# A routed two-layer block on one core: nine of forty expert tiles cut to 128 rows, reads and pads moved in the DMA order

## The chip, the cores and the metric

The kernel runs on one NeuronCore of a Trainium2 chip. Its engines each take their own instructions in order and meet at semaphores: TensorE (PE; its weight loads PEld), VectorE (DVE), ScalarE (ACT), GpSimd (POOL), and SyncE (SP), which here only issues DMAs. The metric is the device time of one execution in microseconds, as a median over runs.

## The reference, cut to what matters

Two layers follow each other on 4096 tokens (32 sequences of 128) of 256 numbers. Each layer has a 16-head cross-attention to a context, and then a feed-forward part in which each token goes to the best two of eight experts.

```
x = x + tanh(g_xattn[0]) * attention0(layernorm(x), ctx)
x = x + tanh(g_ffn[0])   * experts0(layernorm(x))        # relu(x W1 + b1) W2 + b2, hidden 1024
x = x + tanh(g_xattn[1]) * attention1(layernorm(x), ctx, mask)
x = x + tanh(g_ffn[1])   * experts1(layernorm(x))        # (silu(x Wg) * (x Wu)) Wd, hidden 512
```

Each layer so has 8192 rows of expert work (two per token), and their split over the experts is known only while the kernel runs.

## The kernel before, in words

A product in full precision is made of three in the fast format: every operand is cut into a rounded part ("high") and a rest ("low", the original less the rounded part), and `three` (L466 to L470) adds high by high, high by low and low by high. So each operand costs a rounding copy on ACT and a subtraction on DVE or POOL.

The attention of a layer runs in 128 steps (`FIRST`, `START`). While it runs, the router ranks the tokens of each of 8 groups, and POOL scatters their rows by indirect DMAs (L1554) into a buffer in memory, sorted by expert. The last of these steps (`late`, up to `LAST`) lie among the first 13 expert tiles.

The experts take the sorted rows in tiles of `TS` = 256 rows, `NT` = 39 tiles in a layer. Each tile belongs to one expert. The first `KE` = 16 are listed after six groups (`dve_lists_early`); the other 23 after all eight (`dve_lists`, L1366, three parts from step `LIST1` = 171). The 23 are as many as the worst split needs. Tiles past the last real one repeat it, and their rows are scattered out of bounds, so that nothing is written. Behind each expert's rows `pad` (L855) writes 256 rows that point nowhere, so that a tile may read past the end.

Per tile i the engines do this, each in its own order:

- PE (`pe_experts`, L687): turns the rows of tile i+1 (`pe_turn_x`, four transposes, L638), then the up products of tile i in four groups q (`pe_up`, 48 matmuls of 256 columns), then the down products of tile i-1 in two halves (`pe_down`, 48 matmuls in layer 0, 24 in layer 1). "Iteration i" below is this stretch, from one group of L638 to the next.
- ACT (`act_experts`, L915): in layer 1 the scaling of tile i-2's output (`act_y`, L882); the rounding of weight quarter 3 of tile i-1 (`act_w`, L865); relu with bias (L895) or silu (L898) of each group; the rounded hidden part (L906, L908); the rounded rows (L871); and quarters 0 and 1 of tile i+1 and quarter 2 of tile i.
- DVE (`dve_experts`, L1461): in layer 0 the output plus bias of tile i-2 (`dve_y`, L1440); the rests of the hidden parts (L1446, L1449); in layer 1 silu times up (`dve_gated`, L1455); the rests of the rows (L1417); and by `low_w` (L1413) the rests of weight quarters 1 and 2.
- POOL (`pool_experts`, L1584): `low_w` of quarter 3 of tile i-1, the late scatters, two scatters of tile i-2's output rows (`pool_y`, L1579, in layer 1 L1581), and `low_w` of quarter 0 of tile i+1.
- SP (`sp_experts`, L1728): the DMAs, in one order: rows of tile i+2 (`sp_fetch_x`, L1635), in layer 0 two biases, then weight quarter 3 of tile i, quarters 0 and 1 of tile i+2, quarter 2 of tile i+1. The raw quarters have one buffer each, so a fetch waits until the rest of the quarter before it is made. At tile 13 (`KE - 3`) SP issues all eight pads in a row, and in layer 0 at tile 18 three weight reads and two context reads for the next layer.

The weights' rounded parts and rests (`WH`, `WL`) exist once: the up half may be replaced when the up products that read it are done, and so with the down half. The rows' buffer `xt` and the rounded rows `XS` exist twice.

Of the kernel before, what the change touches and what calls it, by code (L numbers as in the profile page):

```python
# [6 lines left out]
F32 = mybir.dt.float32  # L7
# [8 lines left out]
T = B * S  # L16
E = 8
# [5 lines left out]
NT = (2 * T - E) // TS + E  # L23
GE, KE = 6, 16
assert KE <= -(-(2 * GE * G * S - E * (TS - 1)) // TS)
# [20 lines left out]
C_TOK = C_TILE + NT - KE  # L46
# [4 lines left out]
def constants():  # L51
# [9 lines left out]
    c[:, C_TILE:C_TILE + NT - KE] = np.arange(NT - KE)  # L61
# [52 lines left out]
LIST0, TX, LIST1 = 116, (124, 126), 171  # L114
# [51 lines left out]
def step(s, name):  # L166

    for b in range(B):
        if s == (START + LATE_AT[name][b] if b in LATE_AT[name] else 4 * b + AT[name]):
            return b  # L170
    return None

# [7 lines left out]
def program(nc, A):  # L180
    ctx = ExitStack()
    with ctx:  # L182
# [60 lines left out]
        tl = sb("tl", [128, 4, E])  # L243
        tli = sb("tli", [128, 2, E], I32)
# [62 lines left out]
        tile2 = [(L, i, a) for L in LL for i in range(NT) for a in range(2)]  # L307

# [13 lines left out]
        d_fy = [mark(f"d_fy{r}", [k for k in tile2 if k[1] % 2 == r], 16) for r in range(2)]  # L322
# [132 lines left out]
        def experts_out(w, L):  # L455

            w.wait_ge(*m_dn[L, NT - 1, 1])
            w.wait_ge(*m_y[L][L, NT - 1, 1])
            w.wait_ge(*v_h[L, NT - 1, 3])
            w.wait_ge(*p_w3[L, NT - 1])  # L460
            w.wait_ge(*d_fy[(NT - 1) % 2][L, NT - 1, 1])
            w.wait_ge(*d_fy[NT % 2][L, NT - 2, 1])
# [169 lines left out]
        def pe_turn_x(e, w, L, i):  # L632
            bank = place[L, "tx", i]
            w.wait_ge(*d_fx[i % 2][L, i])
            bank_free(w, L, "tx", i)
            for t in range(2):
                for a in range(2):
                    ins = e.transpose(bank[:, t * 256 + a * 128:t * 256 + (a + 1) * 128], xt[:, i % 2, a, t * 128:(t + 1) * 128], ident)  # L638
            ins.then_inc(*m_x(L, i))

        def pe_up(e, w, L, i, q):
            w.wait_ge(*v_x[L, i])
            w.wait_ge(*l_w[q // 2][L, i])
            if i:
                w.wait_ge(*(v_h[1, i - 1, q] if L else a_h[0, i - 1, q]))
            else:
                w.wait_ge(*(a_p[L, NU - 3], a_p[L, NU - 2], a_p[L, NU - 1], a_pt[L, NU - 1])[q])
            for z in range(2):
                f = q if L else 2 * q + z
                for t in range(2):  # L650
                    c = t * (F0, F1)[L] + f * 128 + z * L * 2 * F1
                    ins = three(e, HBK[q][:, z * 256:z * 256 + 256], (WH[:, c:c + 128], WL[:, c:c + 128]),
                                (XS[i % 2][:, 0, t * 256:t * 256 + 256], XS[i % 2][:, 1, t * 256:t * 256 + 256]), t == 0, t == 1)
            ins.then_inc(*m_h(L, i, q))

        def pe_rows(e, w, L, i, f, a):
            nf, c = NFs[L], (2 * F0, 4 * F1)[L] + f * D
            w.wait_ge(*v_h[L, i, f if L else f // 2])
            w.wait_ge(*l_w[2 + 2 * f // nf][L, i])
# [3 lines left out]
        def pe_down(e, w, L, i, half):  # L663
            nf = NFs[L]
            if i:
                w.wait_ge(*m_y[L][L, i - 1, 1])
# [3 lines left out]
            for f in range(half * nf // 2, (half + 1) * nf // 2):  # L670
                for a in range(2):
                    ins = pe_rows(e, w, L, i, f, a)
            ins.then_inc(*m_dn(L, i, half))

        def pe_down_last(e, w, L):

            w.wait_ge(*m_y[L][L, NT - 2, 1])
            for a in range(2):
                for f in range(NFs[L]):
                    ins = pe_rows(e, w, L, NT - 1, f, a)  # L680
                ins.then_inc(*m_dn(L, NT - 1, a))
# [5 lines left out]
        def pe_experts(e, w, L):  # L687
# [13 lines left out]
            pe_down_last(e, w, L)  # L701
# [143 lines left out]
        def act_attention(e, w, L):  # L845
            act_first(e, w, L)
            for s in range(FIRST, START):
                act_step(e, w, L, s)
                for i in range(2):
                    if s == TX[0] + i:  # L850
# [16 lines left out]
        def act_turn_x(e, w, L, i):  # L867
# [3 lines left out]
            e.activation(XS[i % 2][:, 0], place[L, "tx", i][:, :], ACT.Copy).then_inc(*a_x(L, i))  # L871

        def act_y(e, w, i):

            w.wait_ge(*v_xi[1, i])
            if i >= 2:
                w.wait_ge(*d_fy[i % 2][1, i - 2, 1])
            else:
                w.wait_ge(*v_xup[1, B - 1])
            for a in range(2):  # L880
                w.wait_ge(*m_dn[1, i, a if i == NT - 1 else 1])
                e.activation(yo[:, i % 2, a], YB[a][:, 0:D], ACT.Copy, scale=xg[:, i % 4, a:a + 1]).then_inc(*a_y(1, i, a))  # L882

        def act_hidden(e, w, L, i, q):
            r = i % 2
# [954 lines left out]
```

## Time and profile before

| what | value |
|---|---|
| median of 3 runs | 1677.26 us (1676.21 to 1680.76) |
| profiled execution | 1675.83 us, its span 1674.0 us |
| mean granted TensorE clock | 0.973 |
| PE, ACT, DVE, POOL busy share | 93%, 74%, 73%, 50% |
| DMA, mean over the span | 153 GB/s |
| layer 0 experts | first group of L638 at 358.51 us, the last at 837.83 us |
| layer 1 experts | first group of L638 at 1244.78 us, the last at 1639.40 us |

The share of a busy engine is read per stage: an engine is the bound of a stage if it stands idle nowhere in it. A timeline row gives in brackets the idle time of the engine before the instruction and what ended it.

### The profile page before, as it was taken

Reading aid. Unit: us, or ns where it says so; the run is one execution under the profiler, and the core shown is the slowest. Engines: PE = TensorE matmul, PEld = TensorE weight load, DVE = VectorE, ACT = ScalarE, POOL = GpSimd, SP = SyncE. Lnnn points to the kernel's source line nnn. Section 1 sums busy time; section 2 is a strip of 40 time slices with the busy share of each in tenths; the row PEclk is TensorE's granted clock in tenths of the full one; section 3 lists DMA queues with packets and bytes.
Section 4 is the critical chain, followed back from the end, with each engine's and each line's share of the span. In section 5 each row is a group of like instructions: output and inputs, shape, how many; then the busy total and the mean of one; then the engine's idle time right before and its main releaser. Section 6 shows DMA issues by size and latency. Waiting matters only on the chain. (4 is left out here: it accounts for less than half of the span.)

```text
span 1674.0 us, 37438 instructions
## 1 busy us (share of the span) xinstructions
PE 1548.8 (93%) x12728; PEld 1404.1 (84%) x12728; DVE 1218.4 (73%) x2778; ACT 1234.4 (74%) x2854; POOL 844.1 (50%) x907
## 2 busy tenths in 40 slices
PE   7999999989999899999988999999989887899996
PEld 5788888869999899999986777777769876899996
DVE  5677777758899677777857788888766867566663
ACT  5888888878877678888854877777777655677774
POOL 4124444345677465555551123333335677677776
PEclk9999999999999999999999999999989998899999
DMA  3212222147677887777742223333246667888783
GB/s 112 54 50 75 76 77 77 52 132 211 206 238 221 228 275 212 231 222 229 231 128 64 71 85 104 103 109 106 61 133 191 164 183 203 219 218 234 224 226 97
DMA packets 208990, 256.57 MB, mean 153 GB/s; under 512 B 29555, under 2 KB 156788, under 8 KB 208800
## 3 DMA queue, kind: packets, MB, share of 16 engines
q1 hardware_dynamic: 187040, 219.53, 44.8%
q0 software_dynamic: 21120, 34.39, 8.1%
q8 instruction: 101, 1.65, 0.4%
q14 instruction: 89, 0.73, 0.1%
q10 hardware_dynamic: 640, 0.26, 0.1%
HBM read 194.53 MB, written 45.74 MB: 144 GB/s over the span
## 5 line engine op out<-in xcount | busy, mean ns | idle before, releaser
L1413 POOL TENSOR_TENSOR KXR<-U,KXR 128x1024 fp32r<-128x1024 f32 (+1 forms) x156 | 356.1, 2285 | 270.1 <-ACT KXR L865 247.4
L468 PE MATMUL ps<-QR,KXR 128*128 128x256 f32 x1248 | 365.2, 293 | 21.7 <-POOL KXR L1413 9.7
L469 PE MATMUL ps<-QR,KXR 128*128 128x256 f32 x1248 | 357.1, 286 | 0.0
L470 PE MATMUL ps<-QR,KXR 128*128 128x256 f32 x1248 | 357.1, 286 | 0.0
L865 ACT ACTIVATE KXR<-U 128x1024 fp32r<-128x1024 f32 (+1 forms) x312 | 288.9, 948 | 88.4 <-PE ps L470 44.3
L803 ACT ACTIVATE U<-ps,mx 128x128 f32<-128x128 f32 x1024 | 299.1, 405 | 17.3 <-DVE mx L1233 16.9
L468 PEld LDWEIGHTS ps<-QR,KXR 128*128 128x128 f32 x1248 | 243.9, 195 | 25.3 <-POOL KXR L1413 10.7
L469 PEld LDWEIGHTS ps<-QR,KXR 128*128 128x128 f32 x1248 | 243.8, 195 | 0.0
L470 PEld LDWEIGHTS ps<-QR,KXR 128*128 128x128 f32 x1248 | 243.2, 195 | 0.0
L1233 DVE TENSOR_REDUCE mx<-ps 128x4 f32<-128x512 f32 x256 | 174.3, 683 | 67.0 <-PE ps L470 35.4
L1413 DVE TENSOR_TENSOR KXR<-U,KXR 128x1024 fp32r<-128x1024 f32 (+1 forms) x156 | 195.0, 1281 | 24.3 <-ACT KXR L865 24.0
L546 PE MATMUL ps<-cst,U 128*128 128x128 f32 x1024 | 164.1, 284 | 11.7 <-DVE U L1243 10.4
L810 ACT ACTIVATE U<-ps 128x512 f32<-128x512 f32 x256 | 166.6, 651 | 6.7 <-PE ps L546 6.7
L1554 POOL DMA_INDIRECT xs_scr<-XR,PI x112 | 113.8, 1016 | 113.5 <-DVE PI L1142 85.6
L546 PEld LDWEIGHTS ps<-cst,U 128*128 128x128 f32 x1024 | 118.2, 144 | 49.3 <-issue 23.0
L895 ACT ACTIVATE U<-ps,b1s 128x256 f32<-128x256 f32 x312 | 130.3, 472 | 28.2 <-PE ps L470 28.2
L468 PE MATMUL ps<-KXR,PTR 128*128 128x256 f32 x480 | 137.6, 287 | 6.2 <-DVE U L1440 3.5
L1446 DVE TENSOR_TENSOR PTR<-U,PTR 128x512 fp32r<-128x512 f32 x80 | 93.5, 1194 | 65.3 <-ACT PTR L906 65.3
L469 PE MATMUL ps<-KXR,PTR 128*128 128x256 f32 x480 | 136.4, 284 | 0.0
L470 PE MATMUL ps<-KXR,PTR 128*128 128x256 f32 x480 | 136.3, 284 | 0.0
L1581 POOL DMA_INDIRECT out<-U,xi x78 | 123.7, 1586 | 20.8 <-issue 20.2
L468 PE MATMUL ps<-KXR,QR 128*128 128x512 f32 x256 | 123.3, 482 | 6.9 <-ACT U L803 3.6
(228 smaller groups left out, 3985.3 us busy)
## 6 DMA issues: line engine op xcount, KB each, us to landing
U<-in_wpack SPq DMA_DIRECT2D x234, 512.0 KB, 4.4
U<-in_wpack SPq DMA_DIRECT2D x78, 256.0 KB, 4.4
KXR<-U SPq DMA_DIRECT2D x504, 32.0 KB
U<-xs_scr SPq DMA_DIRECT2D x39, 258.0 KB, 4.5
U<-xs_scr SPq DMA_DIRECT2D x39, 257.0 KB, 4.6
U<-in_ctx_t SPq DMA_DIRECT2D x16, 512.0 KB, 5.9
U<-ys_scr SPq DMA_DIRECT2D x32, 256.0 KB, 3.2
U<-in_L_ffn_b SPq DMA_DIRECT2D x39, 128.0 KB
```

The source lines that it names most:

```text
L468: e.matmul(o, wh, xh, start=first, stop=False)
L469: e.matmul(o, wh, xl, start=False, stop=False)
L470: return e.matmul(o, wl, xh, start=False, stop=done)
L546: ins = e.transpose(bank[:, h * 128:(h + 1) * 128], PB[:, i % 3, h], ident)
L803: ins = e.activation(PB[:, i % 3, h], SB_[i % 3][:, h * 128:(h + 1) * 128], ACT.Exp, bias=mx[:, i % 4, h:h + 1], scale=-1.0)
L810: e.activation(PT[:, i % 3].rearrange("p h k -> p (h k)"), pt_place["p", i][:, :], ACT.Copy).then_inc(*a_pt(L, i))
L865: e.activation(w_cols(L, WH, n), w_raw(L, n), ACT.Copy).then_inc(*a_w[n](L, i))
L895: ins = e.activation(HB[:, r, f], HBK[q][:, z * 256:z * 256 + 256], ACT.Relu, bias=b1s[:, r, f:f + 1])
L1233: e.tensor_reduce(mx[:, i % 4], SB_[i % 3][:, :].rearrange("p (h k) -> p h k", h=4), AX.X, ALU.min).then_inc(*v_mx(L, i))
L1413: e.tensor_tensor(w_cols(L, WL, n), w_raw(L, n), hi, ALU.subtract).then_inc(*l_w[n](L, i))
L1554: e.indirect_dma_start(xs_d[L], bass.IndirectOffsetOnAxis(ap=PI[:, g % 2, z, j:j + 1], axis=0), xr(g)[:, z, j, 0:ROWS[L]], None).then_inc( ...
L1581: ins = e.indirect_dma_start(ys_d[1], at, yo[:, r, a, :], None, bounds_check=T - 1, oob_is_err=False, compute_op=ALU.add)
```

## The change

Of 40 tiles in each layer 31 hold 256 rows ("pairs" of halves) and nine hold 128 ("singles"): tiles 18, 21, 23, 26, 29, 31, 34, 37 and 39. The row slots of a layer go from 39 x 256 = 9984 to 31 x 256 + 9 x 128 = 9088. The lists name first the pairs, then the singles (`column` maps a tile to its place), in four parts with 40 small DVE instructions in place of three with 20.

For a single, the rounded rows and their rests lie side by side in one 256-column operand. The up products are then two matmuls per weight block instead of three: high by (high, rest) and low by (high, rest), 32 matmuls in all. The two halves of a bank are added afterwards: ACT copies the right half out (`act_part`, with the bias in layer 0), DVE adds the left (`dve_sum`). In layer 1 ACT then makes the silu (`act_gate`) and DVE the product from two SBUF operands. The product of low by rest, left out before, is now within the sum. The down products of a single take one half: 24 matmuls in layer 0, 12 in layer 1.

The rest of the edits: rows are read three tiles ahead instead of two, behind quarter 3; the first two tiles' rows are read behind all four quarters of tile 0, and tile 0's rows are turned one step later (`TX`); the pads go out four each at tiles 11 and 12, between the other reads; the five reads for the next layer go out one each at tiles 18 to 22; and in layer 1 the rest of quarter 3 of tiles 0 to 15 is made on DVE. `pe_down_last`, which did the last tile's two halves of rows one after the other, is dropped. The hidden buffers of even and odd tiles change places.

```diff
-NT = (2 * T - E) // TS + E
+NT, NPAIR = 40, 31
+SINGLES = (2, 5, 7)
-LIST0, TX, LIST1 = 116, (124, 126), 171
+LIST0, W0, TX, LIST1 = 116, 124, (125, 126), 171
+def single(i):
+    return i >= KE and (i - KE) % 8 in SINGLES
...
+        def l_w(L, i, n):
+            return v_w3 if n == 3 and L == 1 and i < KE else (p_w0, v_w1, v_w2, p_w3)[n]
...
         def pe_up(e, w, L, i, q):
+                    if single(i):
+                        o, xx = HBK[q][:, z * 256:z * 256 + 256], XS[i % 2][:, :, t * 128:t * 128 + 128]
+                        e.matmul(o, WH[:, c:c + 128], xx, start=t == 0, stop=False)
+                        ins = e.matmul(o, WL[:, c:c + 128], xx, start=False, stop=t == 1)
...
+        def act_part(e, w, L, i, q):
+            r, part = i % 2, HBK[q][:, :].rearrange("p (z n) -> p z n", z=2)[:, :, HALF:TS]
+            w.wait_ge(*m_h[L, i, q])
+            w.wait_ge(*v_h[L, i - 2, q])
+            if L == 0:
...
+                    ins = e.activation(HB[:, r, f, HALF:TS], part[:, z], ACT.Identity, bias=b1s[:, r, f:f + 1])
+            else:
+                ins = e.activation(HB[:, r, 4 + q].rearrange("p (z n) -> p z n", z=2), part, ACT.Copy)
+        def act_gate(e, w, i, q):
+            w.wait_ge(*v_s[1, i, q])
+            e.activation(HB[:, i % 2, 4 + q, 0:HALF], HB[:, i % 2, q, 0:HALF], ACT.Silu).then_inc(*a_h(1, i, q))
...
         def act_experts(e, w, L):
+                for q in range(4 if single(i) else 0):
+                    act_part(e, w, L, i, q)
+                    if q == 0 and i + 1 < NT:
+                        act_turn_x(e, w, L, i + 1)
+                    if q == 1 and i + 1 < NT:
+                        act_w(e, w, L, i + 1, 0)
+                    if L == 0 and q:
+                        act_hidden_high(e, w, 0, i, q - 1)
+                    if L == 1 and q:
+                        act_gate(e, w, i, q - 1)
+                    if L == 1 and q > 1:
+                        act_hidden_high(e, w, 1, i, q - 2)
...
+        def dve_sum(e, w, L, i, q):
+            r, part = i % 2, HBK[q][:, :].rearrange("p (z n) -> p z n", z=2)[:, :, 0:HALF]
+            w.wait_ge(*a_t[L, i, q])
+            if L == 0:
+                hb = HB[:, r, 2 * q:2 * q + 2]
+                ins = e.tensor_tensor(hb[:, :, 0:HALF], part, hb[:, :, HALF:TS], ALU.add)
+            else:
+                o, t = (HB[:, r, f].rearrange("p (z n) -> p z n", z=2) for f in (q, 4 + q))
+                ins = e.tensor_tensor(o, part, t, ALU.add)
         def dve_gated(e, w, i, q):
+            if single(i):
+                left, right = HB[:, r, 4 + q, 0:HALF], HB[:, r, q, HALF:TS]
...
         def dve_experts(e, w, L):
+                if L == 1 and 1 <= i <= KE:
+                    low_w(e, w, 1, i - 1, 3)
+                for q in range(4 if single(i) else 0):
+                    dve_sum(e, w, L, i, q)
+                    if q == 0 and i + 1 < NT:
+                        dve_turn_x(e, w, L, i + 1)
+                    if L == 0 and q:
+                        dve_hidden(e, w, 0, i, q - 1)
+                    if L == 1 and q:
+                        dve_gated(e, w, i, q - 1)
+                    if L == 1 and q > 1:
+                        dve_hidden(e, w, 1, i, q - 2)
...
         def pool_experts(e, w, L):
-                if i:
+                if i and (L == 0 or i > KE):
                     low_w(e, w, L, i - 1, 3)
...
         def sp_experts(e, w, L):
+            sp_fetch_x(e, w, L, 2)
             for i in range(NT):
+                x, m = 4 * (i - KE + 5), i - KE - 2
-                if i == KE - 3:
-                    for x in range(E):
-                        pad(e, w, L, x)
-                if L == 0 and i == KE + 2:
-                    sp_ahead(e)
-                    for g in range(2):
-                        sp_context(e, w, 1, g)
-                if i + 2 < NT:
-                    sp_fetch_x(e, w, L, i + 2)
...
                 if i:
                     sp_fetch(e, w, L, i, 3, sp_expert(e, w, L, i))
+                if x in (0, 4):
+                    pad(e, w, L, x)
+                if i + 3 < NT:
+                    sp_fetch_x(e, w, L, i + 3)
+                if x in (0, 4):
+                    pad(e, w, L, x + 1)
+                if L == 0 and 0 <= m < 3:
+                    sp_ahead(e, m)
+                if L == 0 and 3 <= m < 5:
+                    sp_context(e, w, 1, m - 3)
...
```

## Rows read from the trace of the kernel before

**Rows 1.** The page's first part, and one group of its fifth (count | busy us, mean ns).

```profile
PE 1548.8 (93%) x12728; PEld 1404.1 (84%) x12728; DVE 1218.4 (73%) x2778; ACT 1234.4 (74%) x2854; POOL 844.1 (50%) x907
...
L803 ACT ACTIVATE U<-ps,mx 128x128 f32<-128x128 f32 x1024 | 299.1, 405 | 17.3 <-DVE mx L1233 16.9
```

**Rows 2.** Stretches: length; busy PE, PEld, DVE, ACT, POOL (count); clock, DMA share, GB/s.

```profile
706.69:754.39 47.70, 47.70 (x403) 47.70 (x402) 35.85 (x41) 39.34 (x68) 28.31 (x16) 1.00 0.79 226
1512.37:1557.74 45.37, 45.37 (x383) 45.37 (x382) 31.56 (x66) 34.49 (x76) 34.20 (x20) 1.00 0.83 229
```

**Rows 3.** PE timeline at one boundary of layer 0 (start, us, engine, line).

```profile
718.36 0.28 PE L469 MATMUL ps<-KXR,WR 128*128 128x256 f32 x1
718.48 0.28 PE L470 MATMUL ps<-KXR,MK 128*128 128x256 f32 x1
718.59 0.60 PE L638 MATMUL ps<-cst,U 128*128 128x128 f32 x4
```

**Rows 4.** The view of rows 2, of disturbed iterations: two, two, two, two, one, one, one.

```profile
536.35:570.49 34.14, 26.26 (x202) 25.85 (x201) 19.42 (x19) 19.44 (x34) 16.41 (x9) 0.90 0.88 243
606.41:635.15 28.74, 25.57 (x202) 25.36 (x201) 21.25 (x23) 19.66 (x34) 14.63 (x8) 0.94 0.87 287
1407.12:1438.85 31.73, 19.90 (x154) 19.49 (x153) 14.88 (x27) 14.00 (x31) 16.41 (x9) 0.84 0.83 207
1377.33:1407.12 29.79, 22.40 (x154) 21.58 (x153) 25.14 (x63) 15.74 (x34) 22.77 (x17) 0.83 0.72 185
1339.31:1358.14 18.83, 12.58 (x92) 12.35 (x93) 6.51 (x15) 9.26 (x19) 16.61 (x12) 0.82 0.67 174
...
358.51:365.26 6.75, 5.12 (x38) 4.11 (x38) 2.98 (x6) 4.04 (x9) 0.52 (x1) 0.58 0.87 273
1244.78:1250.72 5.94, 4.85 (x33) 3.73 (x33) 2.04 (x5) 4.04 (x9) 0.37 (x1) 0.50 0.94 306
```

**Rows 5.** PE timeline: first transposes of three tiles, idle time and its releaser in brackets.

```profile
556.58 1.12 PE L638 MATMUL ps<-cst,U 128*128 128x128 f32 x4 [7.11 <-DMA U<-xs_scr]
...
1428.40 0.90 PE L638 MATMUL ps<-cst,U 128*128 128x128 f32 x3 [10.32 <-DMA U<-xs_scr]
...
621.65 0.66 PE L638 MATMUL ps<-cst,U 128*128 128x128 f32 x4 [3.17 <-DMA U<-xs_scr]
```

**Rows 6.** SP timeline of layer 0: the eight pads, and two neighbouring reads of a steady tile.

```profile
541.04 8.74 SPq L858 DMA_DIRECT2D xs_scr<-cst  x8
...
709.10 0.38 SPq L1635 DMA_DIRECT2D U<-xs_scr  x1
710.25 0.35 SPq L1616 DMA_DIRECT2D b1s<-in_wpack  x1
```

**Rows 7.** Timelines of a steady layer-1 iteration (from 1539.59): ACT one row, then POOL.

```profile
1540.60 0.63 ACT L865 ACTIVATE KXR<-U 128x512 fp32r<-128x512 f32 x1
...
1541.31 1.29 POOL L1413 TENSOR_TENSOR KXR<-U,KXR 128x512 fp32r<-128x512 f32 x1 [1.77 <-ACT KXR L865]
1542.76 1.55 POOL L1581 DMA_INDIRECT out<-U,xi  x1 [0.15 <-issue]
1544.61 1.55 POOL L1581 DMA_INDIRECT out<-U,xi  x1 [0.30 <-issue]
1545.62 2.99 POOL L1413 TENSOR_TENSOR KXR<-U,KXR 128x1024 fp32r<-128x1024 f32 x1
```

**Rows 8.** DVE instructions of two lines: duration in ns, least/median/most, first and last start.

```profile
L1446 DVE TENSOR_TENSOR PTR<-U,PTR x80: 658/692/3223, 369.9 to 857.3; 128x512 fp32r<-128x512 f32 x80
...
L1449 DVE TENSOR_TENSOR PTR<-ps,PTR x80: 410/420/426, 1258.6 to 1655.9; 128x256 fp32r<-128x256 f32 x80
```

**Rows 9.** POOL timeline of layer 1 during the late scatters.

```profile
1334.11 1.22 POOL L1554 DMA_INDIRECT xs_scr<-XR,PI  x1 [6.21 <-DVE PI L1142]
1335.36 1.29 POOL L1413 TENSOR_TENSOR KXR<-U,KXR 128x512 fp32r<-128x512 f32 x1
```

**Rows 10.** DVE timeline of layer 0: an instruction of the late list's first part.

```profile
512.21 2.99 DVE L1376 CAST tl<-tli 128x8 f32<-128x8 int32 x1
```

More of the change, by code:

```diff
@@ L45 @@
 C_TILE = C_LT + 64
-C_TOK = C_TILE + NT - KE
+C_TOK = C_TILE + max(KE, NPAIR - KE)
 C_PAD = C_TOK + 2 * B
@@ L171, in step, with halves, column @@
     return None
+def single(i):
+    return i >= KE and (i - KE) % 8 in SINGLES
+def halves(i):
+    return range(1 if single(i) else 2)
+def column(i):
+    if i < KE:
+        return i
+    n = sum(single(m) for m in range(i))
+    return NPAIR + n if single(i) else i - n
+assert sum(not single(i) for i in range(NT)) == NPAIR and single(NT - 1)
+assert 2 * NPAIR + NT - NPAIR == 2 * T // HALF + E - 1
 def late(i, k):
@@ L700, in pe_experts @@
                     pe_late(e, w, L, i, 2 + half)
-            pe_down_last(e, w, L)
+            for half in range(2):
+                pe_down(e, w, L, NT - 1, half)
         def act_weight(e, w, L, i):
@@ L1305, in dve_step @@
                     dve_lists_early(e, w, L, n)
-            for n in range(3):
+            for n in range(4):
                 if s == LIST1 + n:
@@ L1366, in dve_lists @@
         def dve_lists(e, w, L, part):
-            n, lt, ti = CR[:, B], cst[:, C_LT:C_LT + 64].rearrange("p (a b) -> p a b", a=E), cst[:, C_TILE:C_TILE + NT - KE]
+            n, lt, ti = CR[:, B], cst[:, C_LT:C_LT + 64].rearrange("p (a b) -> p a b", a=E), cst[:, C_TILE:C_TOK]
+            np_, nl = NPAIR - KE, NT - KE
+            pairs, ends, cuts, sums, over, rest, du, dp, ds = (tl[:, m] for m in range(9))
             if part == 0:
                 w.wait_ge(*v_c.now)
-                e.tensor_tensor(tl[:, 3], CR[:, B], cst[:, C_REG:C_REG + E], ALU.add).then_inc(*v_c.up())
-                e.tensor_scalar(tli[:, 0], n, float(TS - 1), None, ALU.add).then_inc(*v_c.up())
+                e.tensor_tensor(sums, CR[:, B], cst[:, C_REG:C_REG + E], ALU.add).then_inc(*v_c.up())
+                e.tensor_scalar(tli[:, 0], n, float(HALF - 1), None, ALU.add).then_inc(*v_c.up())
@@ new lines, in dve_lists @@
+                e.tensor_tensor(tlm[:, :, :], tl[:, 5:6, :].to_broadcast([128, E, E]), lt, ALU.mult).then_inc(*v_c.up())
+                e.tensor_scalar(du, du, float(TS), float(REG), ALU.mult, ALU.add).then_inc(*v_c.up())
+                w.wait_ge(*v_c.now)
+                e.tensor_reduce(sums, tlm[:, :, :], AX.X, ALU.add).then_inc(*v_c.up())
+                e.scalar_tensor_tensor(ds, rest, float(-HALF), du, ALU.mult, ALU.add).then_inc(*v_c.up())
+                w.wait_ge(*v_c.now)
+                e.tensor_scalar(pairs, ends, -1.0, None, ALU.add).then_inc(*v_c.up())
@@ L1571, in pool_y @@
             if i:
-                w.wait_ge(*d_fy[1 - r][L, i - 1, 1])
+                w.wait_ge(*d_fy[1 - r][L, i - 1, end(i - 1)])
             elif L == 1:
                 w.wait_ge(*d_out[NG - 1])
-            for a in range(2):
+            for a in halves(i):
                 w.wait_ge(*m_y[L][L, i, a])
@@ L1720, in sp_attention @@
                     v = sp_expert(e, w, L, 0)
-                    for n in range(2):
+                    for n in range(4):
                         sp_fetch(e, w, L, 0, n, v)
@@ L1724, in sp_attention @@
                         sp_fetch_x(e, w, L, i)
-                    for n in range(2, 4):
-                        sp_fetch(e, w, L, 0, n, v)
         def sp_experts(e, w, L):
```

224 lines of the change are left out of this document (138 added, 86 removed).

## The prediction

> **What bounds the kernel now.** The busy shares come first: PE 93%, no other engine above 74% [rows 1]. A share is a mean over stages, so the expert stages are read next, in stretches. In layer 0 four undisturbed iterations take 47.70 us and PE is busy for 47.70 of them, so an iteration is 11.92 us of PE; in layer 1 five take 45.37, all PE, 9.07 each [rows 2]. The reader is to see two things there: PE has no gap, and ACT comes second with 9.83 us an iteration in layer 0 and 6.90 in layer 1. The boundary gives the price of one matmul of 256 columns, 0.12 us from start to start [rows 3]: 96 of them at 0.119 make 11.42 in layer 0 and the turn of the next rows the other 0.5; 72 make 8.57 in layer 1, and the turn 0.5.
>
> Then the disturbed iterations. A pair of layer 0 takes 34.14 where two quiet ones take 23.84, another 28.74; in layer 1 there are pairs of 31.73 and 29.79 where two take 18.14, and one iteration of 18.83 [rows 4]. The PE timeline says what ends the idle time: rows of a tile that are not there, with 7.11, 10.32 and 3.17 us of idleness [rows 5]. The clock falls with it: 0.82 to 0.94 in all these stretches, against 1.00 in quiet ones, so 1.2 GHz for a part of each.
>
> **The change part by part.** The sum is made against the profiled execution, 1675.83 us (a span of 1674.0 and 1.83 around it); the median of the runs shown is 1.4 more.
>
> *Singles, PE alone.* A single has 32 up matmuls, and 24 down in layer 0 or 12 in layer 1, all of 256 columns: 56 x 0.119 + 0.25 (two transposes instead of four) = 6.9 us, and 44 x 0.119 + 0.25 = 5.5. Nine singles replace eight pairs. Layer 0: 9 x 6.9 - 8 x 11.92 = -33. Layer 1: 9 x 5.5 - 8 x 9.07 = -23.
>
> *Singles in layer 0, with the others.* An iteration with a single's up and a pair's down is 0.45 + 3.8 + 5.7 = 10.0 us of PE; the next, with a pair's up and a single's down, 9.0. The pair's ACT work is 9.83 and does not shrink, so behind each single ACT is up to 1 us late, and the quarters of weights come after it. A single's ACT work: four quarters 4, eight copies of 128 columns at 0.29 (299.1 over 1024, [rows 1]) 2.3, roundings and the turn about 1.8, together 8.1, so it catches up in the iterations that hold one. DMA: a pair moves 226 GB/s x 11.92 us = 2.7 MB [rows 2], a single about 0.25 less (half of the rows in and out), so five pairs and three singles 20.8 MB in 80 us, 260 GB/s; one stretch has 287 at a share of 0.87 [rows 4], so it fits. I take 5 us of the 33 as lost: -28. Bounds: -33, and 0 if every single costs what a pair costs per unit replaced (9 at 10.6).
>
> *Singles in layer 1, with the others.* Here a chain stands beside PE that the change does not shorten. From the boundary at 1539.59: ACT scales the output, then rounds quarter 3 (1540.60); POOL makes its rest (1541.31), two scatters, and from 1545.62 the rest of quarter 0, which ends at 1548.61 [rows 7]. That is 9.02 us after the boundary, and the next up products, at 9.07 + 0.4, need it. PE has 0.4 us of slack today. With a single's up and a pair's down PE needs 0.46 + 3.81 + 2.86 = 7.1 us, while the chain still has a pair's two scatters: PE waits 0.9 to 1.5. In the next iteration PE needs 7.6, but ACT comes late to the chain's first step: a single gives it about 7.8 us (four copies, four silus, four roundings on top of the same quarters), and its last product and rounding wait for DVE. The DVE row without a PSUM operand reaches from 658 to 3,223 ns, the one with it stays between 410 and 426 [rows 8]; the single's product reads SBUF twice, and POOL's rest of quarter 0 lies in the same microseconds, so the last of its products may be held for up to 2.99 us. So the chain starts 2 to 3.5 late, and PE waits another 1.2 to 2.8. I take 3.2 for both waits together: 9 x 3.2 = 29. Waits of this length are where the clock may fall: in the iteration of 18.83 the shortfall is 0.18 x 18.83 = 3.4 us of full speed [rows 4], half of it beside an idle PE; 1.7 us each for four of the waits, 7. Sum: -23 + 36 = +13. Bounds: -23 (all hidden) and +31 (6 us a single).
>
> The Trainium skill (GPSIMD Engine Reference, section Specifications) says that GpSimd shares its SBUF interfaces with VectorE and contends with DVE instructions that have two SBUF inputs. By that rule the old product, which read PSUM, was free of it and each of the new ones may be held, so all nine singles would stand at the upper end of the 2 to 3.5 us and the sum at 1631; without the rule they stand at the lower end and the sum at 1621. The two lines of [rows 8] agree with it.
>
> *Pads.* The eight pads take SP from 541.04 to its next read at 550.61 [rows 6], and the rows queued behind them come 7.11 and 10.32 late [rows 5]. Cost now: 34.14 - 23.84 = 10.3 in layer 0 and 31.73 - 18.14 = 13.6 in layer 1 [rows 4]. Spread by four, each adds 1.15 us of SP (709.10 to 710.25, [rows 6]) to an iteration with 7 reads in layer 0 and 5 in layer 1, so 12.7 and 10.4 us of SP against 11.9 and 9.1: about 1 us late, in iterations that are longer than that anyway. What is late next are tile 16's rows, which wait for the last pad to land and hold quarters 0 to 2 of later tiles behind them. I take 3 us back: -21. Bounds: -24 and -8.
>
> *Rows three ahead, reads spread.* The rows were issued 2.4 us into an iteration for the next one; now they have a whole iteration more. The stretch with the five extra reads costs 28.74 - 23.84 = 4.9 [rows 4], and layer 1 has some 3 us of shorter waits for rows. -8; bounds 0 and -8.
>
> *First tile.* The first tile's iteration has a clock of 0.58 in layer 0 and 0.50 in layer 1 [rows 4]: PE waits for rows that follow the landing of the scatters. Turning them one step later puts one attention step of about 3 us in front of that wait, and the quarters no longer queue behind it: -5; bounds 0 and -10.
>
> *Quarter 3 on DVE.* In layer 1 POOL stands before a scatter for 6.21 us while a ready rest of 1.29 is queued behind it [rows 9]; the iteration of 18.83 [rows 4] comes of that. The change takes 1.29 from POOL and adds 0.7 to DVE, which makes the numbers that the scatter waits for. -3; bounds -10 and +3.
>
> *The lists.* Twenty more small DVE instructions a layer at about 0.2, half of them in a chain; one of the old ones took 2.99 behind POOL [rows 10]. The first part stands in front of `dve_y` in layer 0. +3; bounds 0 and +6.
>
> *The end.* The last tile is a single: its down products are in the sum above; one scatter of 1.55 less: -2.
>
> Sum: -28 + 13 - 21 - 8 - 5 - 3 + 3 - 2 = -51. 1675.8 - 51 = 1625, against the median 1626.
>
> **The rivals.**
> A: PE stays the bound in layer 1 too, the singles save 18 instead of losing 13. For: POOL is busy only 6.8 of 9.07 us an iteration there. Against: the chain of [rows 7] has 0.4 us of slack. 1626 - 31 = 1595.
> B: the singles save nothing in layer 0 as well, by ACT's order or by the reads: 1626 + 28 = 1654. For: ACT's 9.83 beside 9.0. Against: 10.0 of PE on the other side of it.
> C, the slower one: the hand-overs between ACT and DVE inside a single. If in both layers two of a single's four groups are held for 2.99, as the worst row of L1446 shows, each of the 18 singles costs 6 us above PE's time: 1676 - 56 - 36 + 108 = 1692. It decides from 5.1 us a single on, where the 92 us of gains are spent. Against it: the sums read PSUM, like the line that stays at 410 to 426 [rows 8], and up products and down products of a tile lie an iteration apart.
> D: the reads do not come earlier, because the rows' wait on the turn of two tiles before is what holds them: pads and reads give 5 instead of 29: 1650.
>
> **How the numbers follow.** Forecast 0.50, A 0.20, B 0.15, D 0.09, C 0.06. The likeliest gives 1626 us. A reaches below and B and D above; the range 1594 to 1657 takes them in and leaves out C and the outer ends of A. The measurement tells 0.3%, 5 us, from no change. Faster are the forecast, A, B and D, 0.94; of C 0.02 falls within 0.3% and 0.04 beyond it, slower.
>
> **What would show it.** Right: in layer 0 iterations of about 10.0 and 9.0 us around each single with PE nearly always busy; in layer 1 waits of PE for POOL's L1413 (now another line) of 1 to 3 us behind each single, and a granted clock below 1.00 there; no wait for rows above 1 us; tiles 14 to 16 as long as their neighbours. Wrong: layer-1 iterations of 7.1 and 7.6 without waits (A); layer-0 iterations of 11 to 12 behind singles (B); DVE instructions of a single with 2 us and more (C); waits for rows as before (D).

## The result, and the profile after

The changed kernel takes 1663.5 us (median of 4 runs, 1661.6 to 1667.6) against 1677.1 before: a ratio of 0.992, interval 0.989 to 0.994. It is faster by 13.6 us (0.8%), where the forecast was 51, and lies 37 us above the predicted time.

First the page's busy shares of the kernel after, as in [rows 1]:

```profile
PE 1507.7 (91%) x12256; PEld 1357.2 (81%) x12256; DVE 1289.6 (77%) x2920; ACT 1224.8 (74%) x2913; POOL 819.7 (49%) x881
```

PE lost 41 us of work and only 8.5 us of span, so waits took the place of products. DVE is busy for 71 us more. Both are told apart by stretches. The view is that of [rows 2] (length; busy PE, PEld, DVE, ACT, POOL; clock, DMA share, GB/s), cut at the turns of tiles 0, 14, 18 and the last one of layer 0, then of tiles 0, 11 and 17 of layer 1, and the end. Before:

```profile
358.51:536.35 177.84, 167.64 (x1387) 164.84 (x1387) 147.18 (x243) 137.35 (x241) 112.87 (x81) 0.97 0.71 210
536.35:594.35 58.00, 50.12 (x403) 49.71 (x401) 39.94 (x38) 38.47 (x68) 30.77 (x17) 0.94 0.85 239
594.35:837.83 243.48, 240.31 (x2003) 240.03 (x2002) 186.63 (x205) 197.09 (x341) 142.53 (x80) 0.99 0.79 233
1244.78:1367.80 123.02, 106.11 (x848) 102.26 (x849) 84.56 (x223) 80.50 (x167) 76.10 (x60) 0.94 0.67 187
1367.80:1447.92 80.12, 60.80 (x459) 59.23 (x458) 54.64 (x130) 43.63 (x95) 50.75 (x33) 0.87 0.77 198
1447.92:1674.03 226.11, 211.97 (x1770) 211.19 (x1768) 143.65 (x297) 159.65 (x348) 162.47 (x96) 0.98 0.73 202
```

After:

```profile
359.49:539.02 179.53, 167.85 (x1383) 165.74 (x1383) 151.24 (x262) 135.41 (x235) 113.45 (x80) 0.97 0.71 208
539.02:588.97 49.95, 48.24 (x403) 47.81 (x402) 38.26 (x42) 39.08 (x68) 30.17 (x16) 1.00 0.90 262
588.97:817.46 228.49, 217.32 (x1790) 215.07 (x1789) 204.69 (x232) 186.59 (x354) 145.47 (x77) 0.99 0.84 249
1225.79:1340.69 114.90, 102.89 (x844) 99.91 (x845) 88.30 (x233) 76.81 (x160) 62.88 (x50) 0.97 0.72 199
1340.69:1412.60 71.91, 60.25 (x459) 58.97 (x458) 52.72 (x155) 44.89 (x96) 41.92 (x26) 0.93 0.79 217
1412.60:1665.47 252.87, 203.84 (x1576) 199.13 (x1574) 187.09 (x347) 162.03 (x390) 158.68 (x90) 0.93 0.67 182
```

The reader is to see three things. The pads' stretches (the second and the fifth) are 8 us shorter each. The one with layer 0's singles (the third, 21 iterations in place of 20) is 15 us shorter. The one with layer 1's (the last) is 27 longer: PE has 8 us less work there, and 49 us outside of its work instead of 14, DVE is busy for 187 us instead of 144, and the clock is 0.93.

PE's waits, by what ended them (total us, times, longest; "issue" is a wait whose releaser the trace doesn't name):

```profile
PE ps L503 <- issue: 32.7, 15, 4.5
PE ps L503 <- POOL KXR L1515: 13.6, 7, 4.6
PE ps L691 <- issue: 12.6, 6, 3.3
...
PE ps L675 <- DMA U<-xs_scr: 8.7, 2, 4.4
```

The waits for rows of [rows 5] are gone but for the first tile of each layer (two, 4.4 at most). Of the 21 unnamed ones 17 stand ahead of an iteration's first up product in the tiles from the first single on; the other four lie in the pads' stretches. Where they end is seen by laying the engines' timelines side by side. Layer 0:

```profile
664.07 0.60 PE L675 MATMUL ps<-cst,U 128*128 128x128 f32 x4
667.66 2.41 POOL L1515 TENSOR_TENSOR KXR<-U,KXR 128x1024 fp32r<-128x1024 f32 x1 [5.17 <-ACT KXR L900]
670.23 1.25 POOL L1720 DMA_INDIRECT ys_scr<-U,xi  x1 [0.15 <-issue]
671.79 1.44 POOL L1720 DMA_INDIRECT ys_scr<-U,xi  x1 [0.30 <-issue]
673.24 2.37 POOL L1515 TENSOR_TENSOR KXR<-U,KXR 128x1024 fp32r<-128x1024 f32 x1
...
675.71 0.35 PE L503 MATMUL ps<-QR,KXR 128*128 128x256 f32 x1 [2.19 <-issue]
```

Layer 1, two iterations that follow one another:

```profile
1486.40 2.39 POOL L1515 TENSOR_TENSOR KXR<-U,KXR 128x1024 fp32r<-128x1024 f32 x1 [1.22 <-ACT KXR L900]
1486.55 2.40 DVE L1579 TENSOR_TENSOR ps<-U 128x128 f32<-128x128 f32 x1 [0.73 <-ACT U L953]
1488.99 0.28 ACT L963 ACTIVATE PTR<-ps 128x128 fp32r<-128x128 f32 x1 [2.00 <-DVE ps L1579]
...
1498.11 4.16 POOL L1515 TENSOR_TENSOR KXR<-U,KXR 128x1024 fp32r<-128x1024 f32 x2
1501.13 0.36 PE L503 MATMUL ps<-QR,KXR 128*128 128x256 f32 x1 [3.08 <-issue]
```

In layer 0 PE starts 0.10 us after GpSimd's rest of quarter 0 (673.24 + 2.37 = 675.61), which stood behind two scatters. The chain began late: GpSimd's rest of quarter 3 starts 3.6 us after the boundary (667.66 - 664.07), where it starts 1.4 us after it in the kernel before (719.99 - 718.59, below). In layer 1 a single's product, 0.29 us elsewhere, takes 2.40 beside such a rest; ScalarE waits 2.00 for it; and an iteration later the rest of quarter 0 (the first of the two at 1498.11) comes 3.08 us late for PE.

### The profile page after: what moved, and what is told of

Same layout as the page of the kernel before. It is cut to its first block and busy times, and to the rows that moved or that the text cites. A ratio compares the mean times of both kernels' runs of the same rounds, so it can differ in the third digit from the quotient of the medians.

```text
span 1665.5 us, 36632 instructions
## 1 busy us (share of the span) xinstructions
PE 1507.7 (91%) x12256; PEld 1357.2 (81%) x12256; DVE 1289.6 (77%) x2920; ACT 1224.8 (74%) x2913; POOL 819.7 (49%) x881
## 5 line engine op out<-in xcount | busy, mean ns | idle before, releaser
L1515 POOL TENSOR_TENSOR KXR<-U,KXR 128x1024 fp32r<-128x1024 f32 (+1 forms) x144 | 342.2, 2402 | 240.0 <-ACT KXR L900 239.2
L900 ACT ACTIVATE KXR<-U 128x1024 fp32r<-128x1024 f32 (+1 forms) x320 | 296.1, 948 | 75.0 <-DMA U<-in_wpack 51.3
L503 PE MATMUL ps<-QR,KXR 128*128 128x256 f32 x992 | 295.8, 298 | 59.3 <-issue 32.7
L504 PE MATMUL ps<-QR,KXR 128*128 128x256 f32 x992 | 288.4, 291 | 0.0
L505 PE MATMUL ps<-QR,KXR 128*128 128x256 f32 x992 | 288.3, 291 | 0.0
L1515 DVE TENSOR_TENSOR KXR<-U,KXR 128x1024 fp32r<-128x1024 f32 (+1 forms) x176 | 232.8, 1354 | 26.8 <-ACT KXR L900 26.3
L503 PEld LDWEIGHTS ps<-QR,KXR 128*128 128x128 f32 x992 | 197.7, 199 | 68.1 <-issue 48.6
L504 PEld LDWEIGHTS ps<-QR,KXR 128*128 128x128 f32 x992 | 198.2, 200 | 0.0
L505 PEld LDWEIGHTS ps<-QR,KXR 128*128 128x128 f32 x992 | 197.8, 199 | 0.0
L581 PE MATMUL ps<-cst,U 128*128 128x128 f32 x1024 | 163.2, 283 | 11.9 <-DVE U L1315 10.6
L1722 POOL DMA_INDIRECT out<-U,xi x71 | 116.9, 1646 | 54.8 <-issue 25.0
L503 PE MATMUL ps<-KXR,WR 128*128 128x256 f32 x444 | 127.3, 287 | 6.4 <-DVE U L1544 6.4
L503 PE MATMUL ps<-KXR,QR 128*128 128x512 f32 x256 | 123.5, 482 | 8.1 <-ACT U L838 4.8
L504 PE MATMUL ps<-KXR,WR 128*128 128x256 f32 x444 | 126.2, 284 | 0.0
L503 PE MATMUL ps<-KXR,PTR 128*128 128x256 f32 x408 | 116.5, 285 | 5.0 <-POOL KXR L1515 2.0
L931 ACT ACTIVATE U<-ps,b1s 128x256 f32<-128x256 f32 x248 | 103.1, 470 | 20.1 <-PE ps L505 18.9
L504 PE MATMUL ps<-KXR,PTR 128*128 128x256 f32 x408 | 115.7, 284 | 0.0
```

The source lines that it names most:

```text
L503: e.matmul(o, wh, xh, start=first, stop=False)
L504: e.matmul(o, wh, xl, start=False, stop=False)
L505: return e.matmul(o, wl, xh, start=False, stop=done)
L581: ins = e.transpose(bank[:, h * 128:(h + 1) * 128], PB[:, i % 3, h], ident)
L900: e.activation(w_cols(L, WH, n), w_raw(L, n), ACT.Copy).then_inc(*a_w[n](L, i))
L931: ins = e.activation(HB[:, r, f, 0:n], HBK[q][:, z * 256:z * 256 + n], ACT.Relu, bias=b1s[:, r, f:f + 1])
```

## The experiments

Two questions: what each part of the change is worth, and what takes the singles' gain. Theory 1: VectorE's instructions with two SBUF operands are held by GpSimd's rests, and only the short iterations feel it. Rivals: the longer way over ScalarE and VectorE in a single, and GpSimd's queue. Lines and tiles are named as in the changed kernel. Behind each time stands its ratio to the kernel before, run beside it, with a 95% interval. The kernel before took 1673.3 to 1677.1 us in the different groups of runs, so a difference of two medians from different groups is good to about 4 us.

**Without singles.** A flag for each layer; without it the layer has 39 pairs and the lists of before, all else is the change.

```diff
+SING = (0, 0)
+NTS = tuple(40 if s else 39 for s in SING)
...
-    return i >= KE and (i - KE) % 8 in SINGLES
+    return SING[L] and i >= KE and (i - KE) % 8 in SINGLES
```

> All of the change except the singles: 39 pairs in both layers, the lists of before. Theory 1 (GpSimd's rests hold VectorE, and only the short iterations of singles feel it): what is left keeps the gains read off the trace after, about 11 us in layer 0 and 12 in layer 1, so about 1653. Rival (the prediction's sum without its singles: -21 -8 -5 -3, and +2 for the end): about 1642.

1644.6 us, 0.981 (0.980 to 0.983): 19 us faster than with the singles. The gain of 32 us is near what the prediction's terms give for this part (-21 -8 -5 -3 = -37, or 35 with the 2 us for the end). Its stretches:

```profile
359.07:533.92 174.85, 165.34 (x1383) 162.76 (x1383) 146.89 (x241) 135.16 (x235) 112.90 (x80) 0.99 0.72 213
533.92:584.73 50.81, 48.65 (x403) 47.90 (x402) 40.99 (x41) 39.35 (x69) 30.03 (x17) 1.00 0.88 250
584.73:823.19 238.46, 238.46 (x2002) 238.46 (x2001) 185.15 (x204) 196.58 (x340) 143.54 (x80) 1.00 0.81 239
1231.62:1346.73 115.11, 104.24 (x845) 101.51 (x845) 87.41 (x233) 76.98 (x160) 62.55 (x50) 0.95 0.73 200
1346.73:1417.76 71.03, 58.84 (x458) 57.60 (x457) 51.92 (x135) 44.72 (x96) 42.37 (x26) 0.95 0.80 221
1417.76:1642.86 225.10, 211.68 (x1770) 211.19 (x1768) 144.18 (x298) 158.91 (x348) 161.01 (x95) 0.99 0.73 202
```

**Singles in layer 0 alone** (`SING = (1, 0)`).

> Singles in layer 0 alone, layer 1 with 39 pairs. By the stages of the two traces the singles save about 9 us in layer 0 with its end and cost about 20 in layer 1: about 1644, faster than the changed kernel by 20 us. The prediction's terms would give 1642 - 28 = 1614; its rival B (singles save nothing in layer 0) the same as the run without singles.

1638.1 us, 0.978 (0.976 to 0.980). So the singles bring 6.6 us in layer 0 and cost 25.4 in layer 1 (1663.5 - 1638.1).

**Thin rests.** GpSimd's rests of quarters 0 and 3 on a few columns; the low parts of those weights are left as the layer's first tile made them.

```diff
-            e.tensor_tensor(w_cols(L, WL, n), w_raw(L, n), hi, ALU.subtract).then_inc(...)
+            o, raw = w_cols(L, WL, n), w_raw(L, n)
+            if i and l_w(L, i, n) in (p_w0, p_w3):
+                o, raw, hi = (t[:, 0:1, 0:16] if n < 2 else t[:, 0:16] for t in (o, raw, hi))
+            e.tensor_tensor(o, raw, hi, ALU.subtract).then_inc(...)
```

> The changed kernel with GpSimd's rests of quarters 0 and 3 cut to 16 or 16 columns of one block for all tiles but the first of a layer (the rest of the low parts of these weights is not computed again); every wait and every signal stays. Theory 1 (these rests hold VectorE's instructions with two SBUF operands for 2.4 to 3.3 us): the holds go, PE's waits of 1.3 to 3.1 us around the singles go in both layers, about 1625. Rival (ACT is late, because a single's way over ACT and VectorE is longer than a pair's): at most 8 us, 1655 to 1663, PE's waits stay at 1.5 to 3.

1569.1 us, 0.936 (0.935 to 0.938): 94 us less than the changed kernel, far more than expected. The two stretches with singles:

```profile
575.71:788.86 213.15, 213.15 (x1791) 213.15 (x1790) 136.74 (x238) 187.62 (x357) 48.41 (x77) 1.00 0.87 268
...
1360.29:1567.36 207.07, 191.09 (x1576) 188.43 (x1574) 137.88 (x347) 160.56 (x390) 79.23 (x90) 0.98 0.82 224
```

In layer 0 PE is busy for the whole stretch. A single passes as many instructions between ScalarE and VectorE here as in the changed kernel, so that way by itself is not the bound: this rival falls. Thin rests shorten GpSimd's queue as well as the holds, so this run does not tell these two apart.

**All rests on VectorE.** The same work, done elsewhere:

```diff
+RESTS = ((0, 3), (0, 3))
...
+        def on_v(L, i, n):
+            return n in (1, 2) or i > 0 and n in RESTS[L] or n == 3 and L == 1 and i < KE
...
+                if i and on_v(L, i - 1, 3):
+                    low_w(e, w, L, i - 1, 3)
...
+                    if q == 2 and i + 1 < NTS[L] and on_v(L, i + 1, 0):
+                        low_w(e, w, L, i + 1, 0)
```

> The changed kernel with the rests of quarters 0 and 3 on VectorE for all tiles but a layer's first, so GpSimd does no rest beside the experts. VectorE gains 0.96 + 0.96 (0.7 in layer 1) us of work an iteration and loses the holds of about 5 us in layer 0 and 2 to 3 in layer 1. Theory 1: 1630 to 1645. Rival (what counts is how many instructions VectorE and ACT have to pass one another, not the holds): VectorE's extra work makes the singles longer, 1665 to 1680.

1593.0 us, 0.951 (0.949 to 0.952), 70 less than the changed kernel and again far below the expectation. About 24 us of the gain lie ahead of the singles: the first stretch of layer 0 takes 167.3 us instead of 179.5, and the two of layer 1 take 106.2 and 67.6 instead of 114.9 and 71.9, while the pads' stretch of layer 0 takes 1 us more. So it is not true that only the short iterations feel GpSimd's rests, as theory 1 had it. (A rest of 1024 columns takes VectorE 1.22 us, not the 0.96 expected.) Then the same **without singles**, which gives their worth where GpSimd does no rest:

> No singles, and the rests of quarters 0 and 3 on VectorE. Theory 1: without holds the singles are worth what PE saves less what is left of waits: in the run with the rests on VectorE layer 0's stretch with singles took 217 us where twenty pairs take 238, layer 1's 176 against 181, so this kernel is 27 us slower than that one, 1620, and 25 faster than without singles alone (1645), from the first 17 tiles of both layers. Rival (the rests on VectorE help by themselves and the singles bring nothing): 1593 to 1600.

1628.3 us, 0.973 (0.972 to 0.975). The stretches of layer 0's and layer 1's singles, first with singles, then with pairs:

```profile
577.48:794.69 217.21, 214.37 (x1790) 213.34 (x1789) 177.89 (x278) 187.99 (x357) 45.82 (x35) 1.00 0.86 263
...
1371.93:1588.64 216.71, 195.46 (x1576) 189.32 (x1574) 174.24 (x395) 160.15 (x391) 69.89 (x43) 0.98 0.79 215
```

```profile
576.69:815.16 238.47, 238.47 (x2003) 238.47 (x2002) 176.86 (x242) 196.68 (x340) 63.60 (x40) 1.00 0.79 235
...
1399.19:1623.88 224.69, 211.55 (x1770) 211.14 (x1768) 173.23 (x344) 157.30 (x349) 78.53 (x50) 0.98 0.74 204
```

Here the singles are worth 35 us (1628.3 - 1593.0): 21 in the stretch of layer 0 and 8 on the way from it to layer 1 (403.5 against 411.5), 8 in layer 1. VectorE, with 101 us of rests in that stretch of layer 0, is busy for less of it than in the changed kernel (178 us against 205).

**The product from PSUM.** In layer 1 the sum goes back to PSUM and the silu reads it there (not shown), so a single's product has one SBUF operand:

```diff
-                o, t = (HB[:, r, f].rearrange("p (z n) -> p z n", z=2) for f in (q, 4 + q))
-                ins = e.tensor_tensor(o, part, t, ALU.add)
+                t = HB[:, r, 4 + q].rearrange("p (z n) -> p z n", z=2)
+                ins = e.tensor_tensor(part, part, t, ALU.add)
...
-                left, right = HB[:, r, 4 + q, 0:HALF], HB[:, r, q, HALF:TS]
+                left, right = HB[:, r, 4 + q, 0:HALF], up
```

> The changed kernel; in layer 1 a single's sum is written back to PSUM, so its product has one SBUF operand as a pair's has. GpSimd's rests stay. If the held product is what makes layer 1's singles slow, as the prediction had it, most of the 25 us goes: about 1640. If the rest of quarter 1 on VectorE, held behind two rests of GpSimd in a row, is the wait that ends last: 3 to 10 us, 1653 to 1660, and PE's waits of about 3 us behind each single stay.

1640.1 us, 0.981 (0.978 to 0.983), what the held product was to give. GpSimd's work and order are those of the changed kernel. The groups of layer 1's last stretch (count | busy us, mean ns | idle before), the changed kernel first:

```profile
L1579 DVE TENSOR_TENSOR ps<-U 128x128 f32<-128x128 f32 x36 | 34.9, 968 | 6.5 <-ACT U L953 6.5
```

```profile
L1579 DVE TENSOR_TENSOR ps<-U,ps 128x128 f32<-128x128 f32 x36 | 10.5, 291 | 8.7 <-ACT U L953 8.7
```

24.4 us of the product's holds are gone, and 23.4 us of time (19 by the two ratios to the kernel before). That the two numbers agree so well is in part luck, since other holds moved too: VectorE's rests of 1024 columns (quarter 1) took 39.8 us in this stretch instead of 54.1, those of 512 columns 26.5 instead of 18.9. The stretch falls from 253 us to 227, as long as with pairs (225) and still 20 above the thin rests (207).

**One rest each.** `RESTS = ((3,), (3,))`, then `((0,), (0,))`:

> The change's own step carried on: quarter 3's rest on VectorE for all tiles of both layers, GpSimd keeps quarter 0's. Theory 1: half of the held time goes, and two rests of GpSimd never follow one another: 1620 to 1635. Rival (VectorE's added work costs as much as it frees): 1655 to 1665.

> The counterpart: quarter 0's rest on VectorE for all tiles but a layer's first, GpSimd keeps quarter 3's as in the changed kernel. Theory 1: as much as with quarter 3 in layer 0, where both have 1024 columns, more in layer 1, where quarter 0 is twice as long and stands behind the scatters: 1605 to 1625. If it is GpSimd's being late for PE, and not the holds, that counts, all the gain is here and none with quarter 3: 1595 against 1660.

1625.8 us, 0.971 (0.970 to 0.973), and 1599.1, 0.955 (0.954 to 0.957). In layer 0's stretch either is enough (218.0 and 217.0 us); in layer 1's last it is quarter 0 that counts (222.0 against 234.9). Neither "all the gain in quarter 0" nor "half of the holds each" fits both layers, so layer 0 got an experiment of its own.

**Quarter 0 ahead of the scatters.** GpSimd's work stays, its order is turned from tile 16 on; then the same with the product from PSUM.

```diff
                 pool_late(e, w, L, i, 0)
+                if i >= KE and i + 1 < NT:
+                    low_w(e, w, L, i + 1, 0)
                 if i >= 2:
                     pool_y(e, w, L, i - 2)
                 pool_late(e, w, L, i, 1)
-                if i + 1 < NT:
+                if i < KE:
                     low_w(e, w, L, i + 1, 0)
```

> The changed kernel with GpSimd's order turned from tile 16 on: the rest of the next tile's quarter 0 stands ahead of the two scatters instead of behind them. Its work stays, and so do the holds on VectorE. In the changed kernel PE's waits around singles end just as this rest ends, in both layers. If the queue on GpSimd is what makes it late: layer 0's stretch with singles falls from 228 to 215 to 220 us, layer 1's last stretch from 253 to 225 to 235, about 1630. If the holds are (they delay ScalarE's rounding, which this rest waits for): both stretches stay within 4 us, 1655 to 1670.

> The same order, and layer 1's product from PSUM. If queue and held product are two separate costs: layer 1's last stretch falls to 210 to 220 us (PE alone takes 207) and the time is 1610 to 1625. If the order brings nothing: as with the product from PSUM alone, 1637 to 1643.

1641.1 us, 0.981 (0.979 to 0.984), and 1642.6, 0.981 (0.979 to 0.984). The stretches with singles of the first of them:

```profile
588.61:804.82 216.21, 214.69 (x1790) 213.64 (x1789) 185.10 (x235) 185.91 (x356) 143.41 (x78) 1.00 0.87 264
...
1392.20:1636.24 244.04, 200.12 (x1576) 193.05 (x1574) 149.44 (x347) 161.12 (x390) 156.71 (x90) 0.96 0.72 190
```

In layer 0 the order alone gives back 12 of the 15 us over PE's 213. GpSimd's first step of an iteration still comes late there (its rest of quarter 3 starts up to 4.9 us after the boundary, 4.2 in the changed kernel), but without the two scatters ahead of it the rest of quarter 0 is ready in time. So a change of place in GpSimd's queue wins back most of layer 0's loss. It is not shown that the holds had no part in it: against what was expected they did not stay, since VectorE's instructions with two SBUF operands (L1515, L1552, L1554) took 137 us in this stretch instead of 169, and 101 with thin rests.

In layer 1 the order gives 9 us and the product 26, and together no more than the order (245): the two do not add up. What is late there is seen in VectorE's waits in this stretch, with the order alone and then with both:

```profile
DVE xg L1526 <- DMA out<-U,xi: 47.0, 11, 6.2
```

```profile
DVE xg L1526 <- DMA out<-U,xi: 55.4, 18, 5.9
```

VectorE may write new scatter positions and factors (`xi`, `xg`) only when an earlier tile's output rows have landed, and with the scatters one rest later it stands up to 6 us for them; the changed kernel and the one with the product from PSUM have no such wait in this stretch. PE's waits at L503 for VectorE's rests of the hidden parts (L1557) come to 14.6 and 16.8 us there, against 6.4 in the changed kernel. This points to a new chain over the scatters, made by the turned order itself; a kernel without it was not tried.

**Towards a faster version.** Four kernels with all rests of layer 0 on VectorE and the product from PSUM. The first halves the pads:

```diff
-            e.dma_start(xs_d[L][bass.ds(v, TS), :].rearrange("(a p) d -> p a d", a=2),
-                        cst[:, C_PAD:C_PAD + ROWS[L]][:, None, :].to_broadcast([128, 2, ROWS[L]])).then_inc(*d_pad[x](L))
+            e.dma_start(xs_d[L][bass.ds(v, HALF), :], cst[:, C_PAD:C_PAD + ROWS[L]]).then_inc(*d_pad[x](L))
```

> Rests of quarters 0 and 3 on VectorE, the product of a layer-1 single from PSUM, and pads of 128 rows instead of 256 (with singles no list of an expert ends more than 127 rows short). What is left of waits in the run with the rests on VectorE is mostly beside the pads: 51.0 us where four quiet iterations take 47.7 in layer 0, 67.6 where six take 54.4 in layer 1. If the pads' bytes are what the reads of weights wait for: 5 to 10 us less than 1593, 1583 to 1588. If it is their number or their landing: 1590 to 1595. The product from PSUM: nothing, as no rest of GpSimd is beside it.

1590.0 us, 0.949 (0.947 to 0.951). The run with the rests on VectorE alone had 0.951 (0.949 to 0.952), so half of the pads' bytes and the product from PSUM together bring nothing that shows. It is the fastest version here, 73 us below the changed kernel.

> As the half pads, but layer 1's rest of quarter 3 is GpSimd's for tiles 16 and later. VectorE has 0.7 us less an iteration, and the product is free of the hold; the rests of quarters 1 and 2 are not. If the holds of these cost more than the 0.7: 2 to 6 us slower than the half pads; if not: 2 to 4 faster.

(`RESTS = ((0, 3), (0,))`.) 1595.9 us, 0.954 (0.952 to 0.956): slower by 5.9, at the upper end of what was expected.

> As the half pads, and the read of tile 16's rows stands behind the weights' reads of its iteration instead of ahead of them, so its wait for the pads' landing holds no weights back. If that wait is what the tiles after the pads lose (3.7 us before tile 15's up in layer 1, 2.3 in layer 0): 3 to 6 us faster than the half pads. If the reads are slow by the bytes in flight: the same within 2.

```diff
-                if i + 3 < NTS[L]:
+                if i + 3 < NTS[L] and i + 3 != KE:
                     sp_fetch_x(e, w, L, i + 3)
...
+                if i + 3 == KE:
+                    sp_fetch_x(e, w, L, KE)
```

1590.7 us, 0.950 (0.948 to 0.952): the same. The read of tile 16's rows holds back nothing that counts.

> As the half pads, and the rounding of quarter 3 (a copy with one SBUF operand) moves from ScalarE to GpSimd in both layers. ScalarE has 1.06 us less an iteration in layer 0, 0.6 in layer 1. If a GpSimd copy holds VectorE's two-operand instructions as its rests did: 10 to 25 us slower than the half pads, with VectorE's instructions of 0.4 to 0.7 at 1.5 and more. If not: 3 to 8 us faster, since ScalarE is what the pairs behind singles wait for.

```diff
+        def pool_round(e, w, L, i):
+            w.wait_ge(*d_fw[3][L, i])
...
+            e.tensor_copy(w_cols(L, WH, 3), w_raw(L, 3)).then_inc(*a_w[3](L, i))
```

1595.7 us, 0.953 (0.951 to 0.955): 5.7 slower, neither of the two expectations. The copies hold VectorE a little (below); what ScalarE's relief would bring without these holds is not separated.

## Why the prediction was wrong, point by point

*Pads, -21.* The two stretches went from 58.0 to 50.8 and from 80.1 to 71.0 without singles: -16. Right in kind. What is late next was put at 3 us; of the 36 us over quiet iterations in these stretches 20 are left (50.8 against 47.7 of four, 71.0 against six of 9.07), and neither tile 16's rows, which the prediction named for it, nor the pads' bytes made a difference that shows.

*Rows three ahead, -8.* The stretch with the extra reads went from 243.5 to 238.5, all PE; with 1 us in layer 1, -6. Rival D is refuted: no wait for rows is left behind the first tile.

*First tile, -5; quarter 3, -3.* The first tile's iterations of [rows 4] went from 6.75 and 5.94 to 4.22 and 3.42. The wait for the scatters did not shrink (4.0 and 3.3 us before, 4.2 and 4.4 after), so the step that was to hide it did not. Without singles the first fourteen iterations of layer 0 gained 3.0 us and the first eleven of layer 1 7.9; PE's longest wait for GpSimd, beside [rows 9], went from 6.2 to 4.6. The two together are -11 against -8.

*Lists, +3.* Layer 0's first stretch is 4.7 longer with the new lists than with the old (179.5, 174.9). With the rests on VectorE it is not longer (167.3, 168.2). So their number alone does not cost this; that they wait beside GpSimd's rests is likely, but no row here shows it.

*Singles in layer 0, -28.* The step that failed first, and the one with the largest error (21 of the 37 us). They brought 10 in their stretch (238.5 to 228.5) and 6.6 in all, their lists counted. The working asked whether PE, ScalarE and the DMA keep up at 10.0 and 9.0 us an iteration, and put at nothing the chain over GpSimd that it used for layer 1. The trace of before had it:

```profile
719.99 2.40 POOL L1413 TENSOR_TENSOR KXR<-U,KXR 128x1024 fp32r<-128x1024 f32 x1 [4.35 <-ACT KXR L865]
722.55 1.25 POOL L1579 DMA_INDIRECT ys_scr<-U,xi  x1 [0.16 <-issue]
724.11 0.98 POOL L1579 DMA_INDIRECT ys_scr<-U,xi  x1 [0.30 <-issue]
725.10 2.43 POOL L1413 TENSOR_TENSOR KXR<-U,KXR 128x1024 fp32r<-128x1024 f32 x1
```

The boundary is at 718.59 [rows 3]; the rest of quarter 0 ends at 727.53, 8.94 us later. Beside an iteration of 11.92 + 0.5 that leaves 3.5 us, beside one of 9.0 + 0.5 only 0.6, and the prediction itself had ScalarE up to 1 us late there. In the changed kernel the chain starts up to 2.8 us later than its 1.4 after the boundary, and PE waits up to 2.2 us. With the order turned the stretch takes 216 us instead of 228; with no rests on GpSimd the singles are worth 29 us in layer 0, the -28 of the forecast. Rival B, priced at the 28 us, had most of the size and part of the cause. It named ScalarE's order and the reads, and ScalarE is indeed late: in this stretch its roundings of weights wait 19.1 us for reads and its rounded hidden parts 10.7 us for VectorE's sums. But with thin rests the waits for reads are still 10.5 us, the chain still starts up to 2 us late, and PE waits nowhere; what was missing in B is GpSimd's queue between this lateness and PE.

*Singles in layer 1, +13.* The mechanism was right, link by link: a product with two SBUF operands held beside the rest of quarter 0, ScalarE late by it, the chain of [rows 7] late, PE waiting up to 3.1 us behind a single, the clock at 0.93. The size was not: the last stretch costs 27.8 more than with pairs (252.9 - 225.1), the runs 25.4. The waits were put at 29 us in all and the clock at 7; against the thin rests, with the same matmuls, PE stands idle for 33 us more (49.0 against 16.0) and its matmuls take 13 us more (203.8 against 191.1, at a clock of 0.93 against 0.98). Against PE alone (-23) the loss is 51 us, 5.6 a single, near the upper bound of 6 given there. The product took 26 us of it, 8 of the 36 being held for 2.4 to 3.7 us; one held product delays ScalarE's next copy with it (2.00 us in the rows above).

The Trainium skill (GPSIMD Engine Reference, section Specifications) names contention of GpSimd with VectorE's instructions that have two SBUF inputs. The trace agrees, 968 ns on average with two SBUF operands and 291 with one of them in PSUM; by that rule the prediction had all singles at the upper end and the sum at 1631, still too low.

*The others.* Rival A is refuted by the waits, rival C in its size and its place but not in its kind: the sums, which read PSUM, stay at 0.42, but a layer-0 single's rest (L1552, two SBUF operands) was held for up to 3.4 us. The parts that the run without singles holds (pads, rows, first tile, quarter 3) were put at -37, and -32 is what they gave: each is off by 2 to 5 us, and part of the agreement of the sum is luck.

## What to carry to other kernels

When an iteration gets shorter, each chain that runs beside it from one boundary to the next has to be measured in every layer, not only in that where it is nearly late already: with a chain of 8.9 us behind each boundary, cutting 11.9 us of PE to 9.0 uses up the slack. Work that an idle engine does for a busy one is not free when it holds up the busy one; here VectorE did GpSimd's rests in 1.22 us instead of 2.40, and the kernel became 70 us faster with VectorE's busy share at 77% as in the changed kernel. And a part of a change should be timed by itself: this one is 19 us slower than it would be without its main idea, and the same idea is worth 35 us once GpSimd's rests are out of the way.

## What the runs showed of the hardware

By the starts that the trace shows, the engine that starts first is not spared. A VectorE rest of a single (0.42 us elsewhere) that started at 659.51 took 3.27 us beside a GpSimd rest that started 0.57 us later. GpSimd's rest of 1024 columns takes 2.40 us alone; the one from 1498.11 to 1501.04 took 2.93 beside a VectorE rest that started 0.86 us later, but that this one is the reason is not shown.

A GpSimd copy with one SBUF operand holds VectorE too, and for less time: with quarter 3's rounding on GpSimd the longest of VectorE's rests took 2.07 us instead of 1.22, against up to 4.7 beside GpSimd's rests. The copy is also shorter than these (in the median 1.04 us for 1024 columns and 0.63 for 512, where the rests take 2.40 and 1.3), so length and number of operands are not told apart. The copy itself took up to 2.09:

```profile
L1782 POOL CAST KXR<-U x80: 609/1038/2087, 359.6 to 1576.2; 128x1024 fp32r<-128x1024 f32 x40, 128x512 fp32r<-128x512 f32 x40
```
